# A post-layernorm attention and expert kernel: the GpSimd drain at the exit of the block is left out

## The reference

```
bq, bk, bv = sign(bv_q), sign(bv_k), sign(bv_v)
Q, K, V = sign(x * bq), sign(x * bk), x * bv
scores = Q @ K.T / sqrt(256)                     # per sequence, causal
x = layernorm(x + (sigmoid(4 * scores), causal) @ V)

probs = softmax(x @ w_router)                    # 8192 tokens, 32 experts
top1, gate = argmax(probs), max(probs)
slot = top1 * 320 + position among the expert's tokens   # at most 320 are accepted
y[e] = (silu(buf[e] @ w_gate[e]) * (buf[e] @ w_up[e])) @ w_down[e]
x = layernorm(x + (y[slot] * gate if accepted else 0))
```

## Time and profile before

| | us |
|---|---|
| three runs | 556.22, 556.41, 556.51 |
| median | 556.41 |
| profiled execution, span | 556.1 |
| busy in it: PE | 523.5 (94%) |
| busy in it: DVE | 407.6 (73%) |
| busy in it: ACT | 378.5 (68%) |
| busy in it: POOL | 373.8 (67%) |
| last instruction counted as busy | 546.39 to 547.36 |

### The profile page before, as it was taken

One profiled execution on the slowest core, in us unless ns is written; L12 is line 12 of the kernel. 1 busy time (PEld: TensorE's weight loads), 2 busy tenths in 40 slices (PEclk: granted clock), 3 DMA queues, 4 the chain that ended last, 5 costly groups with the idle time before them and its releaser, 6 DMA issues.

```text
span 556.1 us, 12156 instructions
## 1 busy us (share of the span) xinstructions
PE 523.5 (94%) x3990; PEld 458.8 (82%) x4028; DVE 407.6 (73%) x1026; ACT 378.5 (68%) x775; POOL 373.8 (67%) x497
## 2 busy tenths in 40 slices
PE   6999999999999999999999889999999999999970
PEld 5889888898988888988988448888888888888860
DVE  3774878866678857779575637888788888888870
ACT  5886968869778778688686306667667767677640
POOL 4647868777867778786773541677776777676772
PEclk9999999999999999999999999999999999999995
DMA  8994332254332632247911043666777776683200
GB/s 256 374 327 174 82 96 59 82 166 98 115 74 78 165 96 86 62 104 205 317 52 60 18 134 63 187 200 191 214 207 212 204 218 208 210 251 90 61 33 35
DMA packets 91902, 81.52 MB, mean 147 GB/s; under 512 B 31626, under 2 KB 83066, under 8 KB 91840
## 3 DMA queue, kind: packets, MB, share of 16 engines
q1 hardware_dynamic: 84848, 66.39, 41.3%
q0 software_dynamic: 6912, 14.30, 7.6%
q10 hardware_dynamic: 80, 0.07, 0.0%
HBM read 44.33 MB, written 37.90 MB: 148 GB/s over the span
## 4 chain that ended last, share of the span: by engine, by line
PE 84%; DVE 5%; issue 4%; POOL 3%; DMA 1%; ACT 1%; another core or an unknown queue 1%; DVEq 0%; POOLq 0%; SPq 0%; ACTq 0%
PE ps L918 11%; PE ps L919 10%; PE ps L920 10%; PE ps L894 9%; PE ps L1074 8%; PE ps L1082 7%; PE ps L1075 7%; PE ps L1100 5%; PE ps L1108 3%; PE ps L1047 2%; PE ps L937 2%; PE ps L1097 2%; PE ps L1099 1%; PE ps L1098 1%; DVE hl_ring L1170 1%
## 5 line engine op out<-in xcount | busy, mean ns | idle before, releaser
L918 PE MATMUL ps<-v_hl,hl_ring 128*128 128x256 f32 x544 | 175.8, 323 | 0.3 <-DVE hl_ring L1170 0.3
L919 PE MATMUL ps<-v_hl,hl_ring 128*128 128x256 f32 x544 | 153.4, 282 | 0.0
L920 PE MATMUL ps<-v_hl,hl_ring 128*128 128x256 f32 x544 | 153.1, 281 | 0.0
L918 PEld LDWEIGHTS ps<-v_hl,hl_ring 128*128 128x128 f32 x544 | 103.3, 190 | 15.8 <-issue 2.1
L1170 DVE TENSOR_TENSOR hl_ring<-ps,hl_ring 128x512 fp32r<-128x512 f32 (+3 forms) x160 | 93.3, 601 | 20.0 <-ACT ps L695 16.0
L919 PEld LDWEIGHTS ps<-v_hl,hl_ring 128*128 128x128 f32 x544 | 103.6, 190 | 2.4
L920 PEld LDWEIGHTS ps<-v_hl,hl_ring 128*128 128x128 f32 x544 | 103.2, 190 | 0.0
L693 ACT ACTIVATE hl_ring<-ps 128x512 fp32r<-128x512 f32 (+3 forms) x160 | 85.9, 537 | 20.5 <-PE ps L894 9.4
L695 ACT ACTIVATE ps<-ps 128x512 f32<-128x512 f32 (+3 forms) x160 | 87.1, 544 | 0.0
L619 POOL DMA_INDIRECT out_dram<-alone,ids x55 | 69.3, 1260 | 24.5 <-issue 18.8
L535 POOL DMA_INDIRECT expert_rows<-xrow,slot x64 | 64.3, 1005 | 29.2 <-issue 24.9
(11 more groups left out here) (163 smaller groups left out, 1095.8 us busy)
## 6 DMA issues: line engine op xcount, KB each, us to landing
expert_rows<-xs SPq DMA_DIRECT2D x40, 258.0 KB, 5.2
xs<-expert_rows SPq DMA_DIRECT2D x32, 258.0 KB, 3.1
xall<-in_L_attn_x_dram SPq DMA_DIRECT2D x16, 512.0 KB, 4.9
out_dram<-alone SPq DMA_DIRECT2D x16, 512.0 KB
xall<-in_L_ffn_w_gate_dram SPq DMA_DIRECT2D x32, 256.0 KB, 4.5
xall<-in_L_ffn_w_up_dram SPq DMA_DIRECT2D x32, 256.0 KB, 4.7
xall<-in_L_ffn_w_down_dram SPq DMA_DIRECT2D x32, 256.0 KB, 5.1
xs<-expert_rows SPq DMA_DIRECT2D x31, 64.5 KB
```

The lines of the kernel that those rows point to most:

```text
L918: mm(o, ah, v_hl[:, 0, j, :], start=(j == 0 and i % 2 == 0), stop=False, skip_group_check=True)
L919: mm(o, ah, v_hl[:, 1, j, :], start=False, stop=False, skip_group_check=True)
L920: last = mm(o, al, v_hl[:, 0, j, :], start=False, stop=(j == GT * g + i), skip_group_check=True)
```

## The change

The block is opened with an argument more:

```
-        block = ctx.enter_context(nc.Block())
+        block = ctx.enter_context(nc.Block(no_gpsimd_drain=True))
```

## The result

| | before | after |
|---|---|---|
| median of the first comparison, us | 556.46 (4 runs) | 549.57 (4 runs, 549.39 to 549.67) |
| ratio, 95% interval | | 0.9875 [0.9861, 0.9888] |
| span of the profiled execution, us | 556.1 | 547.8 |

What follows compares the result with a forecast made beforehand. The prediction took PE, busy 94% of the span, as the bound, but POOL's DRAIN alone as setting the end: 6.94 + 0.04 = 6.98 us gained, 556.41 - 6.98 = 549.43, forecast 549.4 us, range 548.6 to 550.4.

Steps and rivals of the forecast that it cites:

- The DRAIN is on the path: Kernel's end, from 549.0 us: POOL's DRAIN runs beside no engine or DMA, so removing it gains 6.94 us.
- The hand-over: Between the DRAIN's end and POOL's first semaphore instruction: under 0.1 us, taken as 0.04 us of gain.
- The four added instructions are hidden: Semaphore instructions behind the other engines' DRAINs run under POOL's DMAs, 5.4 us before POOL asks: cost 0.
- The whole and not a part of the DRAIN goes: At POOL's exit: the DRAIN's time belongs to it and isn't hidden work the next instruction must await; gain 6.98 us.
- upper bound: At POOL's exit: gain bounded between 0 and the whole 6.98 us; the prediction took the whole.
- fixed piece of work: One reading of POOL's exit DRAIN: 6.94 us of its own work after 144 indirect DMAs; the other was hidden work.
- Rival A: At the exit: clean-up after indirect DMAs goes on without the DRAIN and holds the end, 556.4 us; chance 4%.
- The 12 ns: Skill's figure for each preamble or postamble DRAIN; by it the change is worth 0.01 us, time staying 556.4.
- Rival B: At the exit: POOL's first semaphore instruction must end some step, so a part stays, 552.2 us; chance 4%.
- rival C: Expert stage: clean-up not done at the end lengthens the next execution's indirect DMAs, up to 582 us; chance 2%.
- The distance between time and span: Outside the span: the runs' median stands 0.3 us above the profiled span, and this stays after the change.
- the marks that hung on it: Signs of being right at the kernel's end: L658 still ends at 548.8 us, the span at about 549.2.

Runs made afterwards that it cites:

- e1: The kernel before, unchanged, run again with its profile: 556.48 us median of 11 runs, ratio 0.9993; profiled execution 556.67 us, span 554.7.
- e4: The changed kernel, unchanged, run again in more rounds beside the kernel before: 549.40 us against 556.40, ratio 0.9875.
- m_drains: Small program without the reference's computation, POOL alone sending batches of indirect DMAs with DRAINs between: 0.13, 0.70 and 5.27 us behind 1, 8 and 64 DMAs.
- e3: The kernel before with a second meeting, a DRAIN on every engine, right behind the first: 556.91 us against 556.63, ratio 1.0004.
- e5: The kernel before, exit DRAIN kept, with a second POOL DRAIN between attention and expert stages: 556.10 us against 556.40, ratio 0.9993.
- e2: The changed kernel with one POOL DRAIN between its last indirect DMA and its wait for the output to land: 555.39 us against 556.63, ratio 0.9973.

## Why the prediction was right

*The DRAIN is on the path, beside nothing, 6.94 us.* Shown: the pair e1 and e4 differs by 7.0 us at one place, while the last DMA and the end of the wait of L658 fall at the same time in both. The hand-over, taken as 0.04 us, is no more than the rounding.

*The four added instructions are hidden.* Shown by the rows of the changed kernel: the latest arrives at 542.2 us, 5.4 us before POOL asks, as worked out.

*The whole and not a part of the DRAIN goes.* This term had been taken at its upper bound because POOL's wait and branch took 43 and 38 ns with DMAs just issued. The bound was right, and so was the reading that nothing hidden holds the next instruction. The reason can now be named: the DRAIN starts its own work, 82 ns for each DMA since the last clearing. It is not the "fixed piece of work" that the prediction spoke of, and not work for all 144 DMAs either, but for 84; why 84 is open. Rival A's evidence, 174 ns for a DRAIN without DMAs ahead of it, was rightly read as "the length comes from the DMAs" (39 to 46 ns in m_drains and e3; the 174 ns at the start are memsets that POOL is still running, the last from 0.40 us), but that doesn't make it work that must be done. The 12 ns that the prediction takes from the Trainium skill (VectorE: DVE Perf Modes, section "The DRAIN you can't avoid") are its figure for DRAINs of the runtime's boilerplate, while L89's belongs to the program itself; four engines' second DRAINs in e3, with nothing left to run, took 7 to 19 ns, and POOL's 6937 ns at the exit are its DMAs'. Rival B gave a gap of 0.2 us and not of some us; rival C's sign, longer indirect DMAs, is absent: median 1111 ns in both. C's idea that such work can fall due between DMAs does hold in the small programs, as one pause of about 3 us for 113 DMAs, not as a price on each.

*The distance between time and span* is the step that failed. The prediction said that the median stands 0.3 us above the span and that this would stay. It is 1.7 to 2.0 us in every execution that has both numbers but one, which has 3.0; the 0.3 compared a late profiled execution with runs that were not late. The forecast came out right in spite of it, since the change left the true distance alone and only the median was carried over, but the marks that hung on it, a span of 549.2 and L658 ending at 548.8 us, were wrong by 1.4 us. That lateness grew between the scatters and the first output (L535's last start 324.7 against 324.2 us, L619's first 347.4 against 346.0) and is one execution's, not the change's: e1 has 323.9 and 346.0 without the change.

## What to carry to other kernels

When the span ends well after the last busy instruction, ask for the sequencer's rows of the line on which the block closes: semaphores, branches and DRAINs are in no busy digit. Removing a GpSimd DRAIN is worth more, the more DMAs GpSimd has issued since the last one; but behind more than 112 DMAs of 128 rows the measured length fell back, so read it from its row. Here POOL waits at L658 until every output DMA has landed, and the exit ran without a DRAIN; no run left out both. Where one must stay, it costs nothing where GpSimd is idle anyway (e5), though e5's did not make the exit's cheap, and 1.2 to 1.5 us less beside the landing of the last transfers (e2).

## What the runs showed of the hardware

- A DRAIN on POOL takes 39 to 46 ns when nothing was issued since the last and nothing runs, and some 82 ns more for each DMA that POOL issued, indirect (of 64 or 128 rows, of 512 to 1032 bytes) or plain (8 of them, 695 ns), up to 112 DMAs of 128 rows (9189 ns).
- A DRAIN's row starts when the sequencer reaches it; behind two queued DMAs it read 10.1 us for 6.9 us of work.
- In the small programs POOL paused for about 3 us ahead of its 114th DMA of 128 rows since the last DRAIN, and ahead of the 129th of 64 rows, and what came before no longer counted in the next one. The full kernel, with 144 DMAs, shows no such pause, and its DRAIN of 6937 ns counts 84.
